# Attention in an audio tower: the inverse row sums are turned by VectorE and spread over partitions through memory instead of by TensorE, and the stage edges are rearranged

## What is computed

```python
q = apply_rope(q)
k = apply_rope(k)
sim = jnp.einsum('bid,bjd->bij', q, k) * scale
sim = jnp.where(causal[None], sim, -jnp.inf)
attn = jax.nn.softmax(sim, axis=-1)
out = jnp.einsum('bij,bjd->bid', attn, v)
...
return out @ Wo + bo
```

## Time and profile before

| quantity | value |
|---|---|
| median of 3 runs | 1666.11 us (1664.1 to 1670.38) |
| the profiled execution's own time | 1669.95 us |
| its span in the trace | 1668.1 us |
| TensorE busy, share of the span | 87% |
| VectorE, ScalarE, GpSimd busy | 71%, 57%, 52% |

### The profile page before, as it was taken

One profiled execution on the slowest core, in us unless ns is written; L12 is line 12 of the kernel. 1 busy time (PEld: TensorE's weight loads), 2 busy tenths in 40 slices (PEclk: granted clock), 3 DMA queues, 4 the chain that ended last, 5 costly groups with the idle time before them and its releaser, 6 DMA issues. The chain is left out here.

```text
span 1668.1 us, 30233 instructions
## 1 busy us (share of the span) xinstructions
PE 1444.7 (87%) x10725; PEld 1359.9 (82%) x10725; DVE 1183.3 (71%) x2575; ACT 952.9 (57%) x2102; POOL 873.5 (52%) x721
## 2 busy tenths in 40 slices
PE   5379999999999999996599999999998847799049
PEld 4269999999999989996499999999998846798039
DVE  6648788888888888784346666666578379459886
ACT  4637676767676767674254444445443335459642
POOL 4458586969686868581355554555544523023000
PEclk8679999999999999998699999999999968899569
DMA  7391202121212120000576766666665331003403
GB/s 254 131 316 54 77 20 83 33 83 33 83 33 83 33 71 17 27 14 29 180 239 191 215 180 193 195 203 203 174 208 156 79 96 47 10 16 124 157 19 112
DMA packets 91427, 186.36 MB, mean 112 GB/s; under 512 B 8997, under 2 KB 64301, under 8 KB 91021
## 3 DMA queue, kind: packets, MB, share of 16 engines
q1 hardware_dynamic: 80765, 170.75, 30.9%
q0 software_dynamic: 10512, 13.68, 4.8%
HBM read 138.57 MB, written 58.91 MB: 118 GB/s over the span
## 5 line engine op out<-in xcount | busy, mean ns | idle before, releaser
L1664 POOL TENSOR_TENSOR expert_w<-expert_raw,expert_w 128x768 fp32r<-128x768 f32 x95 | 182.2, 1918 | 237.5 <-ACT expert_w L1486 237.5
L1444 PE MATMUL psum<-slots_high,expert_w 128*128 128x376 f32 x1216 | 288.5, 339 | 7.2 <-DVE expert_act L1630 5.9
L887 ACT ACTIVATE expert_raw<-psum,neg_max 120x376 f32<-120x376 f32 (+2 forms) x384 | 176.6, 486 | 95.9 <-DVE neg_max L1090 95.9
L1444 PEld LDWEIGHTS psum<-slots_high,expert_w 128*128 128x128 f32 x1216 | 210.6, 190 | 11.4 <-issue 9.6
L1524 ACT ACTIVATE expert_act_high<-expert_act 128x376 fp32r<-128x376 f32 x152 | 78.8, 518 | 181.6 <-DVE expert_act L1630 181.6
L1113 DVE TENSOR_TENSOR pt_low<-psum,pt_high 128x752 fp32r<-128x752 f32 x128 | 120.5, 941 | 81.3 <-ACT pt_high L896 81.1
L1455 PE MATMUL psum<-expert_w,expert_act_high 128*128 128x256 f32 x912 | 172.0, 285 | 3.2 <-ACT slot_out L1506 3.0
L1635 DVE TENSOR_TENSOR expert_act_low<-expert_act,expert_act_high 128x376 fp32r<-128x376 f32 x152 | 110.5, 727 | 79.0 <-ACT expert_act_high L1524 79.0
L1009 POOL TENSOR_TENSOR qk_low<-rotated,qk_high 128x376 fp32r<-128x376 f32 x128 | 126.7, 990 | 66.8 <-ACT qk_high L880 66.7
L1444 PE MATMUL psum<-slots_low,expert_w 128*128 128x376 f32 x608 | 155.5, 337 | 0.0
L1455 PEld LDWEIGHTS psum<-expert_w,expert_act_high 128*128 128x128 f32 x912 | 144.0, 186 | 6.1 <-ACT slot_out L1506 5.7
(11 more groups left out here) (308 smaller groups left out, 3993.6 us busy)
## 6 DMA issues: line engine op xcount, KB each, us to landing
expert_w<-experts_split SPq DMA_DIRECT2D x57, 768.0 KB, 4.3
expert_raw<-in_experts SPq DMA_DIRECT2D x95, 384.0 KB
x_slots<-in_c_slots SPq DMA_DIRECT2D x4, 3102.0 KB
up_spill<-held SPq DMA_DIRECT2D x5, 1128.0 KB, 5.0
held<-up_spill SPq DMA_DIRECT2D x5, 1128.0 KB, 5.8
slot_rows<-x_slots SPq DMA_DIRECT2D x19, 264.0 KB, 4.1
whole_w<-in_experts SPq DMA_DIRECT2D x12, 384.0 KB, 4.5
experts_split<-pt_high SPq DMA_DIRECT2D x12, 384.0 KB
```

Source lines behind the costliest of these rows:

```text
L887: last = act.activation(probs[0:ni, h % 2, at:at + P * it + ni], score_bank(h % 2, it), ACT.Exp, bias=neg_max[0:ni, h % 2, it:it + 1], acc ...
L1444: last = pe.matmul(psum[:, 2 * k + g % 2, 0:TILE_SLOTS], w[hw][:, f, at:at + P], xt[hx][:, i % 2, c, :], start=(n == c == 0), stop=(n == 2 ...
L1664: pool.tensor_tensor(w[1][:, g % RING, :], raw[:, r % RAW, :], w[0][:, g % RING, :].bitcast(F32), ALU.subtract).then_inc(w_low, 1)
```

## The change

The inverse sums are no longer spread and turned on ScalarE and TensorE. The reciprocal is written into the first 6 of 32 columns of a zeroed tile, and VectorE transposes this tile in 32 x 32 blocks: after that, each of the four groups of 32 partitions holds in its first 6 rows the inverses of 32 tokens for 2 heads and 3 tiles. ScalarE's queue stores these with four DMAs (6 rows of 32 numbers each) to a line in memory, and later loads the line back with two DMAs, one per head, each to 64 partitions with the same 376 numbers. `store_inverses(n)` stands at the end of the step before, `load_inverses(n)` in the step itself, between the first exponentials and the second `pt_high`. Five other places change: the waits for the token stage's stores move into attention (at SyncE's start and before the first write of `pt_high` and `pt_low`), `x_low` moves behind the statistics once no new tokens come, SyncE's two kinds of stores swap places, and `keep_running` adds transposes whose result nobody reads at four places of TensorE's list (18, 9 and 70 at the end of attention, 16 at the start of the experts, 14 in the quantised stage).

```diff
+def keep_running(pe, psum, ident, bank, times):
+    for _ in range(times):
+        pe.transpose(psum[:, bank, TOK:TOK + P], ident[:], ident[:])
...
 # tokens_in, SyncE: the x_dram store of batch i-4 now ahead of the h rows of batch i
-                for u in range(2):
-                    sp.wait_ge(x_stored[u], 16 * (BATCH // 2 - 1))
                 sp.wait_ge(tables_in, 16 * 10)
-                for b in range(BATCH - 3, BATCH):
-                    sp.wait_ge(stored[b % 3], 32 * (b // 3 + 1))
...
 # tokens_in, VectorE
-                    if here(i - 4):
+                    if here(i - 4) and here(i):
                         x_low(i - 4)
...
                     if here(i - 2):
                         inverse(1, i - 2, x_made)
+                    if here(i - 4) and not here(i):
+                        x_low(i - 4)
...
 # attention
-        inv_sum = sb("inv_sum", [P, 2, 2, TILES])
-        inv_wide = sb("inv_wide", [P, 2, TILES, P])
+        inv_pad = sb("inv_sum", [P, 2, 32])
+        inv_sum = inv_pad[:, :, 0:2 * TILES].rearrange("p n (u t) -> p n u t", u=2)
+        inv_t = sb("inv_turned", [P, 2, 32])
+        inv_dram = nc.dram_tensor("inv_lines", [2, 2, TILES * P], F32, kind="Internal").ap()
...
 # TensorE: turn
-                    if h % 2 == 0 and 16 * b + h:
-                        pe.wait_ge(inv_kept, 2 * (8 * b + h // 2) - 1)
...
-                    if h % 2:
-                        pe.wait_ge(inv_spread, 8 * b + h // 2 + 1)
-                        last = turn_inverse(b, h // 2, (0, 1))
                     last.then_inc(turned, 1)
 # TensorE: mix
-                        turn_inverse(b, c, (2,))
...
 # TensorE: end
+                pe.wait_ge(proj_read, 16 * BATCH + CR_READ)
+                keep_running(pe, psum, ident, BANK_PROJ, 18)
...
                 logit(LAST)
+                keep_running(pe, psum, ident, BANK_PROJ, 9)
                 ahead_of(LAST)
+                keep_running(pe, psum, ident, BANK_PROJ, 70)
...
 # ScalarE
-                def spread_inverses(b, c):
-                    act.wait_ge(inv_made, 8 * b + c + 1)
-                    act.activation(...)
+                def store_inverses(n):
+                    act.wait_ge(inv_turned, n + 1)
+                    lines = inv_dram[n % 2, :, :].rearrange("u (t q r) -> q (u t) r", t=TILES, r=32)
+                    for q in range(P // 32):
+                        act.dma_start(lines[q, :, :], inv_t[32 * q:32 * q + 2 * TILES, n % 2, :]).then_inc(inv_stored, 16)
+
+                def load_inverses(n):
+                    act.wait_ge(inv_stored, 64 * (n + 1))
+                    if n:
+                        act.wait_ge(o_scaled, n)
+                    for u in range(2):
+                        act.dma_start(inv_rows[HEAD * u:HEAD * (u + 1), :],
+                                      inv_dram[n % 2, u:u + 1, 0:TOK].broadcast_to((HEAD, TOK))).then_inc(inv_in, 16)
...
 # VectorE: inverses and scale_out
                     dve.reciprocal(inv_sum[:, c % 2, :, :], row_sum[:, :, 0:TILES]).then_inc(inv_made, 1)
-                def keep_inverse(b, c):
-                    dve.tensor_copy(...)
+                    dve.wait_ge(inv_made, 8 * b + c + 1)
+                    dve.transpose(inv_t[:, c % 2, :], inv_pad[:, c % 2, :]).then_inc(inv_turned, 1)
...
-                    dve.tensor_copy(inv_rows[:, 2 * P:TOK], turned_inverse(2)).then_inc(inv_kept, 1)
-                    dve.wait_ge(inv_kept, 2 * (8 * b + c + 1))
+                    dve.wait_ge(inv_in, 32 * (8 * b + c + 1))
...
 # expert_tiles and quantised_ffn, TensorE
+                keep_running(pe, psum, ident, 0, 16)
                 turn(0, 0)
...
                 share(STEP_X)
+                keep_running(pe, psum, ident, 0, 14)
```

More of the change, by code:

```diff
@@ L84, in attention_tables, with tokens_in @@
         sb("before", [P, P], BF16), sb("ones_b", [P, P], BF16), sb("slot_base", [P, EXPERTS]))}
-def tokens_in(nc, psum, a, consts, ident, vec, decay, first, weights, h0_rows, x_dram, tables, cos, made):
+def tokens_in(nc, psum, a, consts, ident, vec, decay, first, weights, h0_rows, x_dram, tables, cos, stored, x_stored, made):
     ctx, sb, sem = scopes(nc, made)
@@ L150, in _ @@
                 for i in range(BATCH + 4):
+                    if 2 <= i - 4 < BATCH:
+                        u = (i - 4) % 2
+                        sp.wait_ge(x_kept, i - 3)
+                        sp.dma_start(x_dram[:, :, :, tokens_of(i - 4)], xt[:, u, :, :, :].bitcast(F32)).then_inc(x_stored[u], 16)
                     if here(i):
@@ L368, in _ @@
                         stat(1, i - 2, h[:, (i - 2) % 3, :, :])
+                    if i == BATCH:
+                        masks()
                     if here(i):
@@ L507, in attention @@
          proj_read, swap_made, rope_made, rot_made, qk_high, qk_ready, scores_made, max_made, exp_made,
-         inv_made, inv_spread, inv_kept, o_scaled, turned, pt_high, pt_ready, mixed, o_high, o_ready, out_made, out_kept) = (
+         inv_made, inv_turned, inv_stored, inv_in, o_scaled, turned, pt_high, pt_ready, mixed, o_high, o_ready, out_made, out_kept) = (
             sem(n) for n in
@@ L511, in attention @@
             "proj_read swap_made rope_made rot_made qk_high qk_ready scores_made max_made exp_made "
-            "inv_made inv_spread inv_kept o_scaled turned pt_high pt_ready mixed o_high o_ready out_made out_kept".split())
+            "inv_made inv_turned inv_stored inv_in o_scaled turned pt_high pt_ready mixed o_high o_ready out_made out_kept".split())
         CR_READ, CR_ROT, CR_SCORES, CR_EXP, CR_TURN, CR_PT, CR_MIX, CR_O, CR_QK = 1, 2, 4, 1, 2, 1, 2, 1, 2
@@ L573, in attention, with front_stored @@
         const = lambda name: moe_const(cm, name)
+        def front_stored(engine):
+            for u in range(2):
+                engine.wait_ge(x_stored[u], 16 * (BATCH // 2 - 1))
+            for b in range(BATCH - 3, BATCH):
+                engine.wait_ge(stored[b % 3], 32 * (b // 3 + 1))
         with nc.Block(no_gpsimd_drain=True) as block:
@@ L577, in _ @@
             def _(sp):
+                front_stored(sp)
                 def load_whole(j):
@@ L895, in turned_high @@
                     act.wait_ge(mixed, 16 * b + h + 1)
+                    if b == h == 0:
+                        front_stored(act)
                     act.activation(pt[0][:, h % 2, :, :], psum[:, BANK_PT:BANK_PT + 2, 0:TOK],
                                    ACT.Copy).then_inc(pt_high, 1)
-                def spread_inverses(b, c):
-                    act.wait_ge(inv_made, 8 * b + c + 1)
-                    act.activation(inv_wide[:, c % 2, :, :].rearrange("p t (u n) -> p u t n", u=2),
-                                   inv_sum[:, c % 2, :, :].rearrange("p u (t o) -> p u t o", o=1)
-                                   .broadcast_to((P, 2, TILES, HEAD)), ACT.Copy).then_inc(inv_spread, 1)
+                def store_inverses(n):
[7 more added lines that the diff above has]
+                        act.wait_ge(o_scaled, n)
+                    for u in range(2):
+                        act.dma_start(inv_rows[HEAD * u:HEAD * (u + 1), :],
+                                      inv_dram[n % 2, u:u + 1, 0:TOK].broadcast_to((HEAD, TOK))).then_inc(inv_in, 16)
                 def out_high(b, c):
@@ L976, in step @@
                         qk_split(b, ahead)
+                    if more or c + 1 < PAIRS:
+                        store_inverses(PAIRS * b + c + 1)
                     if c + 1 == PAIRS:
@@ L2386, in audio_tower @@
         front_sems = []
+        front_stored = [ctx.enter_context(nc.semaphore(f"tok_stored{u}")) for u in range(3)]
+        front_x_stored = [ctx.enter_context(nc.semaphore(f"tok_x_stored{u}")) for u in range(2)]
         early = ctx.enter_context(ExitStack())
```

28 lines of the change are left out of this document (8 added, 20 removed).

## The result

The changed kernel takes 1769.88 us (median of 4 runs, 1766.5 to 1776.11) against 1666.61 us for the kernel before on the same chip: a ratio of 1.0618, 95% interval 1.0594 to 1.0642. It is slower by 103 us; 1748 had been predicted, in a range of 1695 to 1830. The profiled execution took 1768.16 us.

What follows compares the result with a forecast made beforehand. The prediction took a ring of waits through ScalarE, VectorE and TensorE, 8.16 us per attention step, as the bound. Attention +93 us and edges -11 gave +82: 1752 us profiled, 1748 us as median, range 1695 to 1830.

Steps and rivals of the forecast that it cites:

- the ring: In attention, the chain of waits from one even head's `pt_high` to the next, through ScalarE, VectorE and TensorE: 8.16 us.
- not TensorE: Rival in attention: TensorE bounds, so removing its transposes gives back 21 us as well, 1633 us; chance 0.06.
- the logits half-step: Attention steps with router logits, 7 batches: `pt_high` waited for the inverse transposes, so 0.22 us come back in each.
- The issue on ScalarE's queue: Six DMA issues per attention step hold ScalarE's queue, 0.45 us each, and delay `pt_high` behind them.
- The rival drawn from it: Issuing on ScalarE's queue is free; only edges and logits steps count: -12.5 us, 1654 us; chance 0.12.
- an issue waits for the running activation: Rival on ScalarE's queue: 2.52 us more per step, 1806 us; chance 0.21 for 1775 to 1835, shared with dearer issues.
- The two terms of the step: In a steady attention step, loads make `pt_high` 0.34 us late and stores 1.25 us: 1.59 us more.
- the bound of 0.38: Lower bound in us per DMA issue on ScalarE's queue; at it, 1.17 us per step and 1723 us.
- The transpose with its hand-over: VectorE's block transpose of 32 columns, which the stores wait for, taken at 0.21 us with the hand-over.
- The last steps of the batches: Attention's 8 last steps of a batch: half of the stores' 1.25 us and the full load, 8 us together.
- The way through memory: Store and load trips in attention are hidden by margins of about 1.8 us; a doubled landing shows little over 0.5 us.
- The edges: Start of attention -8.5 us, its end -1.2, experts' start nothing, quantised stage -1.5; together -11 us, bounds -16 and -4.

Runs made afterwards that it cites:

- Run 4: The kernel before with each of its three inverse transposes made twice: 1675.13 us, ratio 1.005.
- run 5: The changed kernel with the same six DMAs per step issued by SyncE instead of ScalarE, one SyncE load moved: 1665.16 us, ratio 0.9994 to the kernel before.
- run 2: The changed kernel with the two loads issued ahead of the waiting first exponential: 1715.57 us, ratio 1.0286 to the kernel before.
- run 1: The kernel before with moved waits, new `x_low` order, SyncE's order and added transposes, inverse sums left on TensorE: 1655.86 us, ratio 0.993.
- run 6: The changed kernel with loads ahead of the first exponential, one store for four, and the expert rows' clearing behind batch 0's last projection: 1705.72 us.
- run 7: The changed kernel with only the clearing of the expert rows (12 MB) moved behind the last projection of batch 0: 1788.44 us, ratio 1.0748 to the kernel before.

## Why the prediction was right

**The bound.** Right: the ring, not TensorE, sets the step. Run 4 filled TensorE's wait and cost 8 us, not 21; run 5 took the transposes away with nothing in their place on the ring, and the steps stayed at 8.16 us. Only the logits half-step gave 0.22 us back, as said.

**The issue on ScalarE's queue.** Right as a mechanism: run 5 moves the issues to another engine (and one load of SyncE behind the sixth pair) and removes the whole loss of the steady steps, and run 2 removes that of the loads by their place alone. By the page "DMA: Bandwidth & Descriptors" of the Trainium skill, section "Issuing engines are not separate DMA queues", starting a DMA usually takes little beside the DMA itself. The measured 0.31 us for a store and 0.55 us for a load are little beside the 2.7 us to a load's landing, so the rule agrees; but the landing was hidden, and the issue was not. The rival drawn from it falls. So does the one that an issue waits for the running activation: the first load is issued at 520.44, while the exponential of 520.33 still runs.

**The two terms of the step.** 1.59 us were predicted and 0.75 + 0.92 = 1.67 measured, but the parts were off both ways. 0.45 us was taken for every issue: a load takes 0.46 and 0.62, with 0.11 us from the exponential's start to the first and 0.10 behind the second, so 0.75 us instead of 0.34; a store takes 0.31, less than the bound of 0.38, so 0.92 instead of 1.25. That the sum came out near is in part luck. The 0.45 us came from rows in which 0.43 is the commonest length; over the whole trace of the kernel before, 172 of SyncE's issues take 0.33 to 0.36 us and 19 take 0.43. The transpose with its hand-over was taken at 0.21 us; the row has 0.21, and 0.25 pass from its start to the first store. The last steps of the batches and the logits steps were sized nearly right. Without the first step and the scattered ones attention lost 93.9 us, where 93 were predicted.

**The way through memory.** Right for the steady step: a load lands 2.7 us after its issue, and the scaling never waits. Wrong for the first step: the prediction let a bulk transfer of SyncE double a landing and cost half a microsecond. It held the first stores back for some 18 us, and cost 10.3. With the 8.7 us in scattered steps, for which it had no term (near half of them at the low clock), this is most of the 22 us between 1748 and 1769.88. By parts, 93.9 + 10.3 + 8.7 less the 11.2 of the edges is 101.7 of the 103 us between the medians; the rest is within the spread of single executions.

**The edges.** -11 us predicted, -11.2 by run 1. By the stretches of the profile: start of attention -8.55 (-8.5 predicted, as 3.7 for the landing and 4.8 for the moved `x_low`; SyncE's last issue ends at 76.90 and attention starts at 77.71, which makes 3.2 and 5.3); from the last `pt_high` to the experts -2.1 (-1.2); the experts -1.6 (0, within its bound); the quantised stage -2.4 (-1.5). These stretches hold the 3.3 us by which the profiled execution before lies above its median.

## What to carry to other kernels

A DMA that is started from ScalarE's queue costs that queue about 0.3 us for a few rows and 0.6 us for some hundred, as measured here, and this is paid in full by whatever is queued behind it on the ring, however well the transfer itself is hidden. Start it in a place where the engine waits anyway, start one DMA instead of several (its many rows take longer where they meet a bulk transfer, as in run 6), or give it to an engine that is off the ring. Before a short trip through memory is put on a ring, look for the bulk transfer that it will meet, and cut that into pieces that fit between the trips.

## What the runs showed of the hardware

A store of 0.8 KB that met four transfers of 3.1 MB landed only some 18 to 20 us later (the changed kernel and run 7), and one of 128 rows of 128 bytes some 45 us later (run 6), though the bulk was on another engine's queue. By the section "Issuing engines are not separate DMA queues" of the same page of the Trainium skill, DMAs of different engines run on the same 16 DMA engines and interleave. The packet records agree: packets of 128 bytes pass between packets of 49.6 KB, and a DMA has landed only with its last one. What sets the number of lanes, six and four here, no run shows.

An issue overlaps a running activation but not another issue: the first load began 0.11 us behind the start of an exponential of 0.57 us, the second only when the first had ended. And three transposes more or less, which seemed to be work of a full engine, were worth 0.05 us or nothing in a steady step. In the longer steps of the changed kernel, where TensorE is busy for 7.89 of 9.84 us, its clock fell to one half in about a dozen places; in run 5, without the transposes but with steps of 8.16 us, it stood at 1.00 from 140 to 770 us.
